# Three edits to an expert network with a convolution in its middle: how a tile is rounded, when early inputs are asked for, and in which layout the last expert is computed

## The reference

```python
x = x + L0(_gn(x))      # experts, tanh form of gelu
x = x + L1(_gn(x))      # convolution 3x3, 8 channels to 8, edge padding
x = x + L2(_gn(x))      # experts, tanh form of gelu
x = x + L3(_gn(x))      # experts, exact gelu
# x is (B=2, E=8, N=256, D=256) float32
# L0, L2, L3: for each of the 8 experts e
h   = gelu(x[:, e] @ w1[e] + b1[e])   # D=256 -> H=1024
out = h @ w2[e] + b2[e]               # H=1024 -> D=256
# L1: weights are sign(w) * mean(|w|) for each output channel
# _gn: pairs of the 8 channels form 4 groups, mean and variance over (2, 256, 256)
```

## Time and profile before

| | |
|---|---|
| median of 3 runs | 614.26 us (613.71 to 616.48) |
| profiled execution, own time | 611.66 us |
| its span | 609.8 us |
| PE busy | 589.7 us, 97% of the span |
| DVE busy | 427.0 us, 70% |
| ACT busy | 416.7 us, 68% |
| POOL busy | 36.5 us, 6% |
| mean granted PE clock | 0.994 |

### The profile page before, as it was taken

How to read it: one execution, slowest core, us unless ns; L and a number is a source line. 1 busy time by engine, 2 the same in 40 slices (tenths; PEclk the granted TensorE clock), 3 DMA queues, 4 the chain that set the end, 5 groups by cost and what they waited for, 6 DMA issues and landing times.

```text
span 609.8 us, 8503 instructions
## 1 busy us (share of the span) xinstructions
PE 589.7 (97%) x2857; PEld 492.2 (81%) x2857; DVE 427.0 (70%) x888; ACT 416.7 (68%) x706; POOL 36.5 (6%) x57
## 2 busy tenths in 40 slices
PE   8969999999999898999999999999999999999997
PEld 7747888888889776988888888888888888888885
DVE  5747899678658798795966876766766676675532
ACT  4846677667667543697777767777777777777743
POOL 2000000000000562000000000000000000000000
PEclk9979999999999999999999999999999999999999
DMA  8384454555454274432423324223244243244001
GB/s 279 82 280 164 105 156 134 152 147 168 125 145 140 65 155 135 140 139 72 136 70 101 107 69 139 69 74 134 70 119 124 87 130 130 87 124 135 19 18 69
DMA packets 56909, 73.04 MB, mean 120 GB/s; under 512 B 4217, under 2 KB 50459, under 8 KB 56866
## 3 DMA queue, kind: packets, MB, share of 16 engines
q1 hardware_dynamic: 54262, 70.31, 37.9%
q10 hardware_dynamic: 2604, 2.19, 1.5%
HBM read 59.71 MB, written 8.59 MB: 112 GB/s over the span
## 4 chain that ended last, share of the span: by engine, by line
PE 84%; DVE 6%; DMA 5%; ACT 2%; issue 1%; SPq 1%; POOL 1%; DVEq 0%; ACTq 0%; POOLq 0%
PE G L1053 40%; PE ACC L1073 13%; PE ACC L1078 13%; PE ACC L1074 13%; DMA W2raw<-in_L_conv_w 1%; PE ACC L1092 1%; DMA NAT<-in_x 1%; DVE XC L878 1%; DVE Cl L870 1%; DVE BN L727 1%; PE TR L1105 1%; ACT HR L631 1%; DMA W1raw<-in_L_conv_w 1%; DVE W1l L783 1%; DMA XC<-x_scratch 1%
## 5 line engine op out<-in xcount | busy, mean ns | idle before, releaser
L802 DVE TENSOR_TENSOR Hl<-HR,Hh 128x512 fp32r<-128x512 f32 (+1 forms) x208 | 134.6, 647 | 155.0 <-ACT Hh L635 154.0
L631 ACT ACTIVATE HR<-G,BT 128x512 f32<-128x512 f32 (+1 forms) x208 | 136.3, 655 | 138.1 <-PE G L1053 138.0
L1053 PE MATMUL G<-Xh,W1l 128*128 128x512 f32 (+1 forms) x416 | 160.4, 386 | 6.0 <-ACT HR L631 5.9
L1053 PE MATMUL G<-Xh,W1h 128*128 128x512 f32 (+1 forms) x416 | 155.6, 374 | 0.0
L1073 PE MATMUL ACC<-Hh,W2l 128*128 128x512 f32 (+1 forms) x416 | 154.2, 374 | 0.2 <-issue 0.2
L1074 PE MATMUL ACC<-Hh,W2h 128*128 128x512 f32 (+1 forms) x416 | 153.8, 373 | 0.0
L1053 PE MATMUL G<-Xl,W1h 128*128 128x512 f32 (+1 forms) x416 | 151.7, 375 | 0.0
L635 ACT ACTIVATE Hh<-HR 128x512 fp32r<-128x512 f32 (+1 forms) x208 | 124.9, 600 | 6.6
L1078 PE MATMUL ACC<-Hl,W2h 128*128 128x512 f32 (+1 forms) x416 | 121.8, 374 | 0.4 <-DVE Hl L802 0.3
L1053 PEld LDWEIGHTS G<-Xh,W1l 128*128 128x128 f32 x416 | 78.6, 189 | 19.2 <-ACT HR L631 6.6
L1073 PEld LDWEIGHTS ACC<-Hh,W2l 128*128 128x128 f32 x416 | 78.5, 189 | 14.7 <-issue 0.6
(11 more groups left out here) (87 smaller groups left out, 349.4 us busy)
## 6 DMA issues: line engine op xcount, KB each, us to landing
W2raw<-in_L_conv_w SPq DMA_DIRECT2D x23, 1024.0 KB, 5.6
W1raw<-in_L_conv_w SPq DMA_DIRECT2D x34, 512.0 KB, 4.5
W1raw<-in_L_conv_w SPq DMA_DIRECT2D x7, 1024.0 KB, 5.1
XC<-x_scratch SPq DMA_DIRECT2D x16, 304.0 KB, 5.9
x_scratch<-XT SPq DMA_DIRECT2D x16, 256.0 KB
out_x<-OUTT SPq DMA_DIRECT2D x16, 256.0 KB, 2.1
NAT<-in_x SPq DMA_DIRECT2D x6, 512.0 KB, 7.8
XT<-XC SPq DMA_DIRECT2D x16, 112.0 KB
```

Of the source, the lines that this page charges most:

```text
L631: nc.scalar.activation(HR[:, u % 2, 0:n], G1[u % 2][:, 0:n], act_of_layer, bias=BT1[:, f, col:col + 1]).then_inc(gelu_done, 1)
L802: nc.vector.tensor_tensor(Hl[:, u % RING, 0:n], HR[:, u % 2, 0:n], Hh[:, u % RING, 0:n].bitcast(F32), ALU.subtract).then_inc(hlo, 1)
L1053: ins = nc.tensor.matmul(G1[u % 2][:, 0:n], w[:, par, c, col], rhs, start=i == 0, stop=i == len(parts) - 1)
```

## The change

Three edits:

1. ACT's `conv_high` reads `XC` itself and applies scale and shift as it reads (Identity with two per-partition operands), where it read POOL's `CN` before. POOL still makes `CN`; the wait for it moves to DVE's `conv_low`.
2. `load_x(2)` and `load_x(3)` are issued right behind the second half of w2[0], and `load_w2(1)` right behind `load_w1(1)`, ahead of the convolution's ten small transfers.
3. The last expert's second product has the hidden values as the stationary operand and the weights as the moving one, so that it comes out in token layout. The bias is added to the residual early (`add_final_bias`), PE transposes the residual into the same banks (`final_residual`, 8 transposes), and the products accumulate on it (`final_g2`, 12 matmuls a unit, of 256 columns). At the end ACT copies batch 0 and DVE batch 1 to `OUTT`. The last evicts and the last out transposes are gone.

```diff
         def w2_stored(w, E):
-            if E < C:
+            if E < C or E == EXPERTS - 1:
                 return w2_columns(w, E)
...
+            for g in (2, 3):
+                load_x(g)
             load_w1(1)
+            load_w2(1)
             for i in range(C):
                 sp.dma_start(conv_rep[i:PART:C], cw[:, i].rearrange("o a b -> o (a b)").unsqueeze(0)
...
-            load_x(2)
-            load_w2(1)
-            load_x(3)
...
             def store_out(e, b, n):
-                sp.wait_ge(out_evac, 2 * n - 1 + b)
+                if e == C - 1 and b == B - 1:
+                    sp.wait_ge(final_dve, 1)
+                else:
+                    sp.wait_ge(out_evac, 2 * n - 1 + b)
...
             def conv_high(q):
+                b, own = blocks(q)
                 w = tile_width(q)
-                act.wait_ge(cn_done, q + 1)
+                if q == 0:
+                    act.wait_ge(prep, 5 + KS + KS * (KS + 2))
+                if q % TILES == 0:
+                    act.wait_ge(pads, 2 + 2 * b)
+                    act.wait_ge(cst_done, 2 + 2 * b)
                 wait(act, conv_mm, q - HRING + 1)
-                nc.scalar.activation(Ch[:, q % HRING, 0:w], CN[:, q % CRING, 0:w], ACT.Copy).then_inc(chi, 1)
+                nc.scalar.activation(Ch[:, q % HRING, 0:w], XC[:, b, own], ACT.Identity, bias=CST[:, B + b:B + b + 1],
+                                     scale=CST[:, b:b + 1]).then_inc(chi, 1)
...
-            for b in range(B):
-                out_evac_step(EXPERTS - 1, b, (TR, G1[0])[b])
+            act.wait_ge(final_done, 1)
+            act.wait_ge(out_st[0], 16 * (C - 1))
+            nc.scalar.activation(OUTT[:, 0].rearrange("p r d -> p (r d)"), ACC[FINAL % 2][0][:], ACT.Copy
+                                 ).then_inc(out_evac, 1)
...
+            def add_final_bias():
+                e = C - 1
+                for m in range(DC):
+                    at = XT[:, m, e]
+                    nc.vector.tensor_scalar(at, at, BT2[:, LAYERS - 1, e, m:m + 1], None, ALU.add).then_inc(final_in, 1)
...
             def conv_low(q):
                 w = tile_width(q)
                 dve.wait_ge(chi, q + 1)
+                dve.wait_ge(cn_done, q + 1)
...
+                if u == unit(FINAL - 1, 6):
+                    add_final_bias()
...
-            for b in range(B):
-                evict(len(PASSES) - 1, (b,))
+            dve.wait_ge(final_done, B)
+            dve.wait_ge(out_st[B - 1], 16 * (C - 1))
+            nc.vector.tensor_copy(OUTT[:, B - 1].rearrange("p r d -> p (r d)"), ACC[FINAL % 2][B - 1][:]
+                                  ).then_inc(final_dve, 1)
...
+            def final_residual(b):
+                if b == 0:
+                    pe.wait_ge(final_in, DC)
+                    pe.wait_ge(evicted, evicted_by(FINAL - 2))
+                for r in range(NC):
+                    for c in range(DC):
+                        at = r * D + c * PART
+                        nc.tensor.matmul(ACC[FINAL % 2][b][:, at:at + PART].rearrange("p (g i) -> p i g", g=GROUPS),
+                                         XT[:, c, C - 1, b, r * PART:(r + 1) * PART], ident[:],
+                                         start=r == 0 and c == 0, stop=False, is_transpose=True)
+            def final_g2(u):
+                t = u % HT
+                par = PASSES[FINAL][0] % 2
+                pe.wait_ge(hhi, u + 1)
+                if t % 2 == 0:
+                    pe.wait_ge(wlo, split_by(PASSES[FINAL][0], 4 + t // 2))
+                pe.wait_ge(hlo, u + 1)
+                for b in range(B):
+                    for r in range(NC):
+                        own = slice(b * N + r * PART, b * N + (r + 1) * PART)
+                        for i, (high, w) in enumerate(((Hh, W2l), (Hh, W2h), (Hl, W2h))):
+                            ins = nc.tensor.matmul(ACC[FINAL % 2][b][:, r * D:(r + 1) * D], high[:, u % RING, own],
+                                                   w[:, par, t], start=False,
+                                                   stop=t == HT - 1 and r == NC - 1 and i == 2)
+                    if t == HT - 1:
+                        ins.then_inc(final_done, 1)
+                if t < HT - 1:
+                    ins.then_inc(g2_done, 1)
...
-                if u >= 2 and not (p == PC and t < 2):
+                if p == FINAL and t >= 2:
+                    final_g2(u - 2)
+                elif u >= 2 and not (p == PC and t < 2):
                     g2(u - 2)
+                if p == FINAL and t < B:
+                    final_residual(t)
...
             for u in (UNITS - 2, UNITS - 1):
-                g2(u)
-            for b in range(B):
-                out_transpose(EXPERTS - 1, b, (TR, G1[0])[b])
+                final_g2(u)
```

More of the change, by code:

```diff
@@ L64 @@
 UNITS = HT * len(PASSES)
+FINAL = len(PASSES) - 1
 def pass_of(E, b):
@@ L362, in build @@
         out_tr, out_evac = sem("out_tr"), sem("out_evac")
+        final_in, final_done, final_dve = sem("final_in"), sem("final_done"), sem("final_dve")
         out_st = [sem(f"out_st{b}") for b in range(B)]
@@ L652, in give_back, with out_evac_step @@
                                         XC[j * C:(j + n) * C, b, own.stop - 1, 1:N + 1]).then_inc(x2_in[b], 16)
-            def out_evac_step(E, b, src=TR):
+            def out_evac_step(E, b):
                 n = E - 2 * C
@@ L659, in out_evac_step @@
                 nc.scalar.activation(OUTT[:, b].rearrange("p r (c g i) -> p (r c) g i", c=DC, g=GROUPS),
-                                     src[:].rearrange("p (a i g) -> p a g i", i=SPAN, g=GROUPS), ACT.Copy
+                                     TR[:].rearrange("p (a i g) -> p a g i", i=SPAN, g=GROUPS), ACT.Copy
                                      ).then_inc(out_evac, 1)
@@ L1095, in conv_tile, with out_transpose @@
                 ins.then_inc(conv_mm, 1)
-            def out_transpose(E, b, dst=TR):
+            def out_transpose(E, b):
                 n = E - 2 * C
-                pe.wait_ge(evicted, evicted_by(len(PASSES) - EXPERTS + E) + (b * DC if E == EXPERTS - 1 else 0))
-                if dst is TR:
-                    wait(pe, out_evac, 2 * n + b)
+                pe.wait_ge(evicted, evicted_by(len(PASSES) - EXPERTS + E))
+                wait(pe, out_evac, 2 * n + b)
                 for r in range(NC):
@@ L1104, in out_transpose @@
                         at = r * D + c * PART
-                        ins = nc.tensor.transpose(dst[:, at:at + PART], XFIN[:, E % 2, c, b, r * PART:(r + 1) * PART],
+                        ins = nc.tensor.transpose(TR[:, at:at + PART], XFIN[:, E % 2, c, b, r * PART:(r + 1) * PART],
                                                   ident[:])
```

## The result

The changed kernel ran at 606.86 us in the median of 4 runs (605.54 to 611.48), the kernel before at 613.99 (median of 4, 610.41 to 616.48). The ratio is 0.9887 with a 95% interval from 0.9839 to 0.9935: faster by more than 0.5%. The gain between the medians is 7.1 us. The forecast was 606.8 us, by a gain of 7.5 us. Runs more than 1.5% above the fastest of their kernel count in the medians here and in no ratio: 660.01 and 1511.57 us of the kernel before, 979.64 us of the early loads alone, and 612.55 and 613.03 us of the changed kernel in its second set, whose ratio would be about 0.001 higher with them.

The account below looks back on a forecast made before the run. PE, 97% busy, was taken as the bound. Gains of 6.2 (early loads), 0.5 (rounding) and 0.8 (last expert) sum to 7.5 us, off the 614.26 us median: 606.8 us; own range 605.3 to 608.0, full range 604.4 to 610.4.

Parts of the forecast that it names:

- The early loads: Start of kernel: w2 of expert 1 lands earlier, PE reaches the mean at 42.3 us, not 48.49; gain 6.2 us.
- pushed nothing back: Rival at the start: 2 MB of early loads delay w1 of expert 1; gain 1.5 to 2.5, 612.3 us, chance 0.04.
- the named rival: Clock falls in the new hole before the mean, costing 1.6 us: time 608.4 us, chance 0.26.
- the prediction's own signs of being wrong: Next profile: a W1raw wait over 3 us, clock under 1.00 between 40 and 50 us, or PE waiting in last pass.
- My argument from the length of the hole: Before the mean: holes of 1.02 us and less leave the clock alone; w1 landing earlier shortens the new one.
- The rounding: Convolution start: DVE waits for POOL alone before its second Cl, 0.7 us less; gain taken as 0.5 us.
- The price of the new form of the instruction: Per-partition scale and shift on ACT in the convolution: 0.1 us each allowed, 2 us for 20, hidden.
- both reckonings: ACT's extra cost in the convolution, 2 us by gelu rows or 3.7 us by the skill, hidden by idle time.
- The last expert: Last pass and tail: 2.33 us saved, less 0.88 for transposes and 0.64 for matmuls; net gain 0.8 us.
- The strided transposes: Last pass: residual transposes write in strides of 64 elements; at twice the time they cost 0.9 us more.
- that rival: In final_g2, stationary loads stop being hidden; at 0.240 us per matmul 11.5 us more, 618.3 us, chance 0.03.
- The median: Whole kernel: the 7.5 us sum taken off the median of 614.26 us gives 606.8 us.

Follow-up runs that it names:

- second set: The changed kernel unaltered, timed again on one chip beside the kernel before and each edit alone: median 610.21 us, ratio 0.9916.
- 6: Changed kernel with the statistics of experts 2 and 3 one unit earlier on DVE (unit 7), first of two sets: median 606.13 us, ratio 0.9872.
- 7: Changed kernel with the load of w1 for expert 2 issued ahead of the ten small transfers: ratio 0.9879, 6 runs.
- 9: Changed kernel with 9 unread filler matmuls on PE in the hole before the mean over partitions: median 603.66 us, ratio 0.9860.
- the half kernels: Changed kernel and kernel before, each with half the convolution's result not moved from XC back to XT: 602.99 to 606.16 and 609.50 to 613.07 us.

## Why the prediction was right

**The early loads: right, by the steps given.** Forecast: the mean at 42.3 us, gain 6.2. Measured: 42.28 and 42.38 against 48.49, 6.2 and 6.1. Inside it several sizes were off and cancelled. w2 took 5.9 us to land, not 5.1, and ACT waited 0.31 us for it, hidden as the prediction said. `load_w1(2)` was issued at 32.83, not 33.0, took 5.4 us, not 5.1, and ACT waited 0.74 us, not 1.2. PE reached the hole at 40.14, not 39.7, so that it was 2.24 and 2.10 us, not 2.4 to 2.6. `load_x(2)` and `load_x(3)` pushed nothing back: w1 of expert 1 was issued at 21.18 and ACT's wait for it was 1.27 us, where it was 1.44. Alone, these loads gave a ratio of 0.9912, as large as that of the whole change in the same set.

**The clock: the named rival came about in part.** In the first profile the clock fell behind the new hole, in the second it didn't. The price forecast, 1.6 us, is what the two profiles differ by in that unit, 1.60. The forecast took one or the other; the runs do both. A clock under 1.00 between 40 and 50 us was also one of the prediction's own signs of being wrong, and the first profile has it. My argument from the length of the hole, that a shorter one is safer, didn't hold: the clock fell behind 1.77, 1.86 and 2.24 us and stayed up behind 2.10 and 2.19. Near 2 us the length alone doesn't tell.

**The rounding: 0.4 for 0.5 in one pair of profiles, not shown as a gain of its own.** DVE's wait before the second `Cl` fell from 1.19 to 0.67 us, and now it is for POOL, as forecast. From the first `Cl` to the end of the last `XC` it is 33.84 us where it was 34.25 (207.27 to 241.52). The kernel with the last expert alone, without the rounding, has 34.24, and 6, 7 and 9, with it, have 33.32, 33.30 and 33.65, so the direction repeats. But the half kernels show no difference, and the runs of the rounding alone none: what part of it is the wait taken away, and what part the transfers that go on beside it, stays open. The price of the new form of the instruction was mis-sized: I allowed 0.1 us from the gelu rows, but `Ch` went from 0.64 to 0.82 us. The Trainium skill, "ScalarE: Activation LUTs", section "What ACT_TABLE_LOAD costs", has about 93 ns for each pointer operand; two of them are 0.19, and the trace agrees with 0.18. It is hidden as both reckonings said (ACT has 16.75 busy us of 35.50 there).

**The last expert: right, 0.7 for 0.8, by the traces.** From the transposes at 575.28 to the end of the last matmul were 28.85 us before; now, from 575.86 to 606.29, they are 30.43. That is 1.58 us more, forecast 1.52. From there to the end of the span it is 3.41 where it was 5.67: 2.26 saved, forecast 2.33. The strided transposes cost what contiguous ones did, and the loads of the stationary operand stayed hidden: that rival fell. In its own run the same pass was 0.7 us shorter and the span 0.4 us lower; the interval of its ratio includes 1.

**The median: close by luck.** 606.8 against 606.86 is a closer hit than the method can give. The four runs lie between 605.54 and 611.48, and twelve more of the same kernel had a median of 610.21 beside 614.81 of before: 4.6 us of gain, 5.2 by the ratio, where 7.5 was forecast. What supports the mechanism is the pair of undisturbed profiles, 7.3 us apart with each term near its forecast. That the same difference could be taken off a median was assumed: it holds only if both kernels have their accidents equally often. The range of 605.3 to 608.0 that the sum gives itself doesn't come out of its bounds either; these give 605.2 to 608.9.

**What no case held.** The prediction's sum was made for executions without the second hole, and these do come to 602.3 by forecast and 602.5 by trace. That there is a stage in which DVE waits for the way back of batch 0 in some executions and not in others, for 1.3 to 4.1 us and with a fallen clock behind it, was not seen, since the one profile of before was of an execution without it. It costs the changed kernel 5.5 us where it is full, and how often it comes weighs on the median: in the second set nine of its twelve runs lay at 608.73 us or over. For the kernel before it is only inferred, from runs of 615 to 618 us at clocks of 0.985 to 0.990, like the profiled run of the rounding alone (616.21 us, 0.987). What makes the transfers slow in one execution (0.96 busy at 124 GB/s) and not in the next stays open. So does whether the rounding or the earlier loads make it more frequent: it stood in four of the nine profiles taken with the rounding and the full way back and in neither of the two without it, which is too few to tell.

**A better version.** The changed kernel with the statistics at unit 7 is clearly faster than the kernel before and probably faster than the changed one: its ratio to before is 0.9872 in each of two sets, and its span of 600.0 us is 2.5 under the changed kernel's best, with the hole gone. The intervals of the ratios still overlap with the changed kernel's. Nine idle matmuls in the hole gave 0.9860, with fewer runs. The two weren't tried together; as both answer the same hole, I would not expect them to add up.

## What to carry to other kernels

When a wait of 6 us is removed, follow the chain to the next thing that is late and put a number on it: here it was the next load in the same queue, and statistics standing behind it on DVE, worth 2 us more in the profiles and lowest runs when they were moved one unit ahead. A transfer whose buffer is free belongs ahead of small ones that nobody needs yet: here each small one cost the queue 0.6 to 0.75 us of issue. And one profile is one execution: where its own time lies at an end of the runs, take a second before explaining the difference.

## What was not expected of the hardware

A matmul with float32 operands of 128 by 128 leaves two records and takes 0.23 to 0.24 us (18 in 4.18 us, 9 in 2.17), twice what one record shows. The transfers from `XC` to `XT`, in packets of 1 KB from two queues, ran at 124 GB/s with a busy share of 0.96 in one execution and at 154 GB/s with 0.59 in another, of the same kernel at the same point of the stage. And the clock fell in some executions and not in others behind holes of about 2 us, at 1.6 us each time, once behind the shortest of them, and twice more than 1 us after PE had gone on.
